# Edge layers of a graph network on one core: 38 instead of 29 tiles fetched as rows, 45 instead of 54 gathered by matmul

## The reference, cut to what matters

```python
def _gine_layer(x, src, dst, edge_attr, eps, We, be, W1, b1, gamma, beta, W2, b2):
    e = edge_attr @ We + be                      # edge_attr: one number an edge
    m = relu(x[src] + e)
    agg = segment_sum(m, dst, num_segments=N)
    h = ((1.0 + eps) * x + agg) @ W1 + b1
    h = (h - mean(h)) * rsqrt(var(h) + 1e-5) * gamma + beta     # over the nodes
    return relu(relu(h) @ W2 + b2)
```

## Time and profile before

| | us |
|---|---|
| median of three runs | 1023.49 (1018.66 to 1024.08) |
| the profiled execution, its own time | 1026.04 |
| its span, first to last instruction | 1024.3 |
| PE busy in the span | 875.0 |
| VectorE busy | 692.1 |
| ACT busy | 499.2 |
| POOL busy | 333.7 |

### The profile page before, as it was taken

The page is one execution under the profiler, slowest core; times in us unless marked ns, Lnnn a source line. Parts: engine busy times, 40 slices in busy tenths (PEclk is TensorE's granted clock), DMA queues, the critical chain, the costliest instruction groups (busy, mean ns, idle before and its releaser), DMA issues.

```text
span 1024.3 us, 13343 instructions
## 1 busy us (share of the span) xinstructions
PE 875.0 (85%) x3642; PEld 624.8 (61%) x3642; DVE 692.1 (68%) x1228; ACT 499.2 (49%) x966; POOL 333.7 (33%) x286
## 2 busy tenths in 40 slices
PE   3979768678969999974999998999999988999793
PEld 2666245456747777753666765676655865667572
DVE  7997635576964646476887577964898569875414
ACT  2386004344534313345775566754776467743421
POOL 3000724567011123335360255503652064502100
PEclk9989557898969999996999999999999999999897
DMA  4413525878314130414683177812886058721001
GB/s 104 143 32 95 140 77 164 247 206 273 132 42 173 40 114 0 135 62 107 164 202 86 37 180 188 218 42 64 187 221 191 4 142 217 196 55 42 1 1 50
DMA packets 58198, 122.16 MB, mean 119 GB/s; under 512 B 8025, under 2 KB 21627, under 8 KB 58134
## 3 DMA queue, kind: packets, MB, share of 16 engines
q0 software_dynamic: 20048, 52.18, 21.5%
q1 hardware_dynamic: 35061, 63.82, 20.2%
q10 hardware_dynamic: 3024, 5.31, 1.4%
HBM read 105.56 MB, written 15.73 MB: 118 GB/s over the span
## 4 chain that ended last, share of the span: by engine, by line
PE 71%; DVE 16%; ACT 5%; issue 4%; DMA 1%; another core or an unknown queue 1%; SPq 0%; DVEq 0%; ACTq 0%
PE ps L908 14%; PE ps L653 12%; PE ps L885 10%; PE ps L924 6%; PE ps L940 6%; PE ps L847 5%; PE ps L796 5%; PE ps L772 4%; PE ps L755 2%; DVE z_parts L1581 2%; ACT slot_recs L995 2%; PE ps L744 1%; PE ps L645 1%; PE ps L659 1%; PE ps L679 1%
## 5 line engine op out<-in xcount | busy, mean ns | idle before, releaser
L908 PE MATMUL ps<-z_parts,onehot_dst 128*125 128x512 f32 x664 | 207.5, 418 | 12.6 <-DVE z_parts L1581 9.5
L653 PE MATMUL ps<-w,xT 128*125 128x512 f32 x660 | 175.0, 419 | 12.7 <-DVE w L1224 4.9
L1581 DVE SCALAR_TENSOR_TENSOR z_parts<-ps,z_parts 128x512 fp32r<-128x512 f32 x216 | 147.6, 687 | 50.8 <-ACT z_parts L1124 43.3
L1124 ACT ACTIVATE z_parts<-ps 128x512 fp32r<-128x512 f32 x216 | 129.1, 598 | 87.5 <-PE ps L885 78.1
L885 PE MATMUL ps<-x_parts,gather_lhs 128*128 x432 | 143.9, 419 | 32.1 <-DVE x_parts L1558 21.0
L908 PEld LDWEIGHTS ps<-z_parts,onehot_dst 128*125 128x125 f32 x664 | 111.6, 188 | 81.4 <-issue 63.0
L653 PEld LDWEIGHTS ps<-w,xT 128*125 128x125 f32 x660 | 126.5, 197 | 49.2 <-issue 19.9
L604 POOL DMA_INDIRECT gathered<-rel_rows,rowi x83 | 88.6, 1068 | 161.3 <-DMA rel_rows<-x_cur 96.1
L619 POOL DMA_INDIRECT queued<-node_rows,srci x60 | 96.1, 1601 | 104.0 <-ACT queued L1058 88.2
L885 PEld LDWEIGHTS ps<-x_parts,gather_lhs 128*128 128x128 f32 x432 | 81.4, 195 | 65.8 <-issue 48.9
L584 POOL TENSOR_TENSOR w<-w_stage,w 128x512 fp32r<-128x512 f32 x36 | 47.9, 1360 | 179.4 <-ACT w L957 179.4
(11 more groups left out here) (240 smaller groups left out, 1204.1 us busy)
## 6 DMA issues: line engine op xcount, KB each, us to landing
w_stage<-in_weights SPq DMA_DIRECT2D x22, 1024.0 KB
onehot_dst<-onehot_rows SPq DMA_DIRECT2D x80, 250.0 KB
onehot_rows<-onehot_dst ACTq DMA_DIRECT2D x20, 250.0 KB
gather_lhs<-edge_src_rows SPq DMA_DIRECT2D x8, 432.0 KB, 8.6
node_rows<-work SPq DMA_DIRECT2D x20, 160.0 KB, 2.0
queued<-node_rows,srci POOLq DMA_INDIRECT x116
node_rows<-work SPq DMA_DIRECT2D x20, 90.0 KB, 2.0
rel_rows<-rel_rows_out SPq DMA_DIRECT2D x10, 160.0 KB, 1.9
```

Source lines behind the costliest of these rows:

```text
L653: mm = pe.matmul(ps[0:R, bank, :], lt[:, a, k, n * R:(n + 1) * R], w[:, b, k, :], start=first and k == 0 and (a, b) == THREE[0], stop=last ...
L908: mm = pe.matmul(ps[0:R, d, :], S[:, j // SK % SR, j % SK, :], Z[:, g % ZR, a, :], start=False, stop=False, skip_group_check=True)
L1124: nc.scalar.activation(Z[:, g % ZR, HI, :], of, ACT.Relu).then_inc(z_hi, 1)
L1581: v.scalar_tensor_tensor(out=Z[:, g % ZR, LO, :], in0=of, scalar=0.0, in1=Z[:, g % ZR, HI, :].bitcast(F32), op0=ALU.max, op1=ALU.subtract) ...
```

## The change

Two constants are new: `TP` = 45, the number of tiles that PE gathers in an edge layer, and `FL` = `TE` - `TP` = 38, the number that POOL fetches. `TF` and `TL` stay what they were where the tiles are made, counted and one-hot encoded. So tiles 45 to 53, full ones, are now fetched. Their gather columns in `L` are still built and loaded, and not used. `ORDER` becomes 7 tiles of PE, then 38 pairs of one PE tile and one fetched tile. Sets on ACT become 19 a layer (15 before), adds on VectorE 19 (14 before). Sources and signs for the fetches (`srci`, `srcf`, `sgf`) are made for 38 columns.

```diff
+TP = 45
+FL = TE - TP
...
-LEAD = TF - 3 * (TL // 2)
+LEAD = TP - FL
 ORDER = [*range(LEAD)]
-for q in range(TL // 2):
-    a, b = LEAD + 3 * q, TF + 2 * q
-    ORDER += [a, b, a + 1, b + 1, a + 2]
-ORDER += range(TF + TL // 2 * 2, TE)
+for q in range(FL):
+    ORDER += [LEAD + q, TP + q]
 STEP = {t: i for i, t in enumerate(ORDER)}
-SETS = (TL + 1) // 2
-ADDS = TL // 2
+SETS = (FL + 1) // 2
+ADDS = FL // 2
...
-        srci = sb("srci", [P, TL], I32)
+        srci = sb("srci", [P, FL], I32)
...
                     if k >= QR:
-                        gp.wait_ge(z_made, l * TE + STEP[TF + k - QR] + 1)
+                        gp.wait_ge(z_made, l * TE + STEP[TP + k - QR] + 1)
                     gp.indirect_dma_start(Q[k % QR][:, :], None, xb_d, row).then_inc(q_in[k % QR], 16)
...
-                for k in range(TL):
+                for k in range(FL):
                     queue_rows(l, k)
...
                     t = ORDER[i] if i < TE else TE
-                    if t < TF:
+                    if t < TP:
...
-                    while k < TL and STEP[TF + k] - 14 <= i:
+                    while k < FL and STEP[TP + k] - 14 <= i:
                         queue_set(l, k)
                         k += 2
...
-                    v.tensor_scalar(SSL[:, g % 2, k, :], iota5[:, :], sgf[:, t - TF + k:t - TF + k + 1], None,
+                    v.tensor_scalar(SSL[:, g % 2, k, :], iota5[:, :], sgf[:, t - TP + k:t - TP + k + 1], None,
...
-            mixed = dlo[:, LEAD:LEAD + 5 * ADDS].rearrange("p (q m) -> p q m", m=5)
+            mixed = dlo[:, LEAD:TE].rearrange("p (q m) -> p q m", m=2)
             v.tensor_copy(dlo[:, 0:LEAD], dlf[:, 0:LEAD])
-            v.tensor_copy(mixed[:, :, 0:5:2], dlf[:, LEAD:TF].rearrange("p (q m) -> p q m", m=3))
-            v.tensor_copy(mixed[:, :, 1:5:2], dlf[:, TF:TF + 2 * ADDS].rearrange("p (q m) -> p q m", m=2))
-            link(v.tensor_copy(dlo[:, LEAD + 5 * ADDS:TE], dlf[:, TF + 2 * ADDS:TE]))
+            v.tensor_copy(mixed[:, :, 0], dlf[:, LEAD:TP])
+            link(v.tensor_copy(mixed[:, :, 1], dlf[:, TP:TE]))
...
-                    while k < TL and STEP[TF + k] <= i + 2:
+                    while k < FL and STEP[TP + k] <= i + 2:
                         queue_add(l, k)
                         k += 2
```

More of the change, by code:

```diff
@@ L896, in _ @@
                         g = l * TE + j
-                        if r >= TF:
-                            if r == TF or r % PK == 0:
+                        if r >= TP:
+                            if r == TP or r % PK == 0:
                                 rest = rest_word(r // PK)
@@ L901, in _ @@
                         else:
-                            last = max(t for t in ORDER[:min(i, TE - 1) + 1] if t < TF)
+                            last = max(t for t in ORDER[:min(i, TE - 1) + 1] if t < TP)
                             d = field(wd if r // PK == last // PK else old, 6 * (r % PK), 7, NT - 1)
@@ L1056, in queue_set @@
                 if k >= QR:
-                    act.wait_ge(z_made, l * TE + STEP[TF + k - QR] + 1)
-                nc.scalar.activation(Q[k % QR][:, :], WEB[:, :], ACT.Copy, scale=wt[:, TF + k:TF + k + 1])\
+                    act.wait_ge(z_made, l * TE + STEP[TP + k - QR] + 1)
+                nc.scalar.activation(Q[k % QR][:, :], WEB[:, :], ACT.Copy, scale=wt[:, TP + k:TP + k + 1])\
                     .then_inc(q_set, 1)
@@ L1111, in _ @@
                     g = l * TE + i
-                    if t < TF:
-                        act.wait_ge(gat_done, l * TF + t + 1)
+                    if t < TP:
+                        act.wait_ge(gat_done, l * TP + t + 1)
                         of = ps[:, 5 + t % 3, :]
                     else:
-                        c = l * ((TL - 1 - (t - TF) % QR) // QR + 1) + (t - TF) // QR + 1
-                        if (t - TF) % 2 == 0:
-                            act.wait_ge(q_in[(t - TF) % QR], 16 * c)
-                        else:
-                            act.wait_ge(q_add, ADDS * l + (t - TF) // 2 + 1)
-                        of = Q[(t - TF) % QR][:, :]
+                        c = l * ((FL - 1 - (t - TP) % QR) // QR + 1) + (t - TP) // QR + 1
+                        if (t - TP) % 2 == 0:
+                            act.wait_ge(q_in[(t - TP) % QR], 16 * c)
+                        else:
+                            act.wait_ge(q_add, ADDS * l + (t - TP) // 2 + 1)
+                        of = Q[(t - TP) % QR][:, :]
                     if g >= ZR:
@@ L1375, in _ @@
             v.tensor_scalar(rowi[:, :], rowf[:, :], -1.0, 0.0, ALU.add, ALU.max)
-            link(v.tensor_scalar(srcf[:, :], rowf[:, TF:TE], float(N + 1), None, ALU.is_ge))
-            link(v.scalar_tensor_tensor(out=srcf[:, :], in0=rowf[:, TF:TE], scalar=float(2 * N + 1), in1=srcf[:, :],
+            link(v.tensor_scalar(srcf[:, :], rowf[:, TP:TE], float(N + 1), None, ALU.is_ge))
+            link(v.scalar_tensor_tensor(out=srcf[:, :], in0=rowf[:, TP:TE], scalar=float(2 * N + 1), in1=srcf[:, :],
                                         op0=ALU.is_ge, op1=ALU.add))
-            v.scalar_tensor_tensor(out=sgf[:, :], in0=srcf[:, :], scalar=-float(NT * P), in1=ps[:, 7, TF:TE],
+            v.scalar_tensor_tensor(out=sgf[:, :], in0=srcf[:, :], scalar=-float(NT * P), in1=ps[:, 7, TP:TE],
                                    op0=ALU.mult, op1=ALU.add)
-            link(v.scalar_tensor_tensor(out=srcf[:, :], in0=srcf[:, :], scalar=-float(N), in1=rowf[:, TF:TE],
+            link(v.scalar_tensor_tensor(out=srcf[:, :], in0=srcf[:, :], scalar=-float(N), in1=rowf[:, TP:TE],
                                         op0=ALU.mult, op1=ALU.add))
@@ L1563, in queue_add @@
                     v.wait_ge(web_in, 16 * (l + 1))
-                v.wait_ge(q_in[k % QR], 16 * (l * ((TL - 1 - k % QR) // QR + 1) + k // QR + 1))
-                v.scalar_tensor_tensor(out=Q[k % QR][:, :], in0=WEB[:, :], scalar=wt[:, TF + k:TF + k + 1],
+                v.wait_ge(q_in[k % QR], 16 * (l * ((FL - 1 - k % QR) // QR + 1) + k // QR + 1))
+                v.scalar_tensor_tensor(out=Q[k % QR][:, :], in0=WEB[:, :], scalar=wt[:, TP + k:TP + k + 1],
                                        in1=Q[k % QR][:, :], op0=ALU.mult, op1=ALU.add).then_inc(q_add, 1)
```

8 lines of the change are left out of this document (4 added, 4 removed).

## The result

The changed kernel took **1047.85 us** in the median of four runs (1039.9 to 1055.3) against 1023.78 us for the kernel before in its four. The ratio is **1.023**, 95% interval 1.016 to 1.030: slower, by 1.6 to 3.0%. On a second chip, where the kernel before takes 988 us, the repeat gave 1.0196 (1.013 to 1.026). Both kernels have now and then an execution in a slower state; such executions are left out of every ratio. The profiled execution of the changed kernel is the slowest of its four: 1055.3 us, 29.3 us above the profiled execution of before.

The account below looks back on a forecast made before the run. PE and VectorE, both nearly full, were taken as the bound, passing to POOL with the transfers. Pace -6.4 and weight loads +4.5 gave -1.9 us against 1026.04, or 1021.5 us as a median; range 1002 to 1040.

Parts of the forecast that it names:

- the start of a layer: Layers 1 to 3: first fetched tile needed five steps earlier, arriving just in time at 597.15 us in layer 1; cost zero.
- the weight loads: Layers 1 to 3: more fetched tiles delay the 1 MB load after the tenth one-hot group; +1.5 us each, +4.5 us.
- the sum: Whole kernel: -6.4 + 4.5 = -1.9 us against the profiled 1026.04, so 1024.1; as a median 1021.5 us.
- Pace: Mixed part of the four edge layers: 0.84 us a step instead of 0.857, -1.6 us a layer, -6.4 us over four.
- The ends of the range, 0.785 and 0.89: Mixed steps: 0.785 us if only POOL's issue limits, 0.89 by the transfers; -5.7 and +2.2 us a layer.
- I cost this at zero, but its cover is gone: Second fetched tile in layers 1 to 3: no cost, but each 0.5 us late costs 0.5 us in three layers.
- C: Mixed part: transfers become the bound, pace 0.89, plus 3 us at each of three weight loads; +17.6, 1041 us; chance 0.22.
- B: Mixed part: transfers have room, only POOL's issue limits, pace 0.785; -18.4, 1005 us; chance 0.22.
- D: Mixed part: tied engines only change partners, pace stays 0.857, weight stalls grow 2 us in three layers; +4.6, 1028; chance 0.13.
- E: POOL's fetches each held by a VectorE instruction reading two SBUF operands, some 10 us more a layer; 1064 us; chance 0.03.
- Wrong in kind if the layers change by over 4 us each: Four edge layers: a change of over 4 us each, in either sense, would make the forecast wrong in kind.
- if anything outside the four layers moves by more than 2 us: Rest of the program: any move of more than 2 us would make the forecast wrong in kind.

## Why the prediction was wrong

The forecast was 1021.5 us, with 1002 to 1040 as its range, and 1047.85 was measured. Two steps failed: the start of a layer, put at zero, and the weight loads, of which the second in each layer was not in the sum.

- **Pace, -6.4 us: right where nothing disturbs.** 0.84 us a step was forecast, 0.832 measured, adds 3.33 us apart for 3.36; layer 0 gained 1.2 to 1.5 for 1.6. In layers 1 to 3 the calm stretch from 52 to 68 gained even 1.5 us each. The ends of the range, 0.785 and 0.89, both fell.
- **Start of a layer, costed at zero: wrong.** This was the step "I cost this at zero, but its cover is gone". POOL starts 4.4 us after PE, as said, but VectorE goes on 7.2 us after the first issue, not after 5.4: the time at which bytes are through was taken for the time at which their reader may go on. The trace of before had a better number: the last recorded landing of a layer's second fetch is there 6.5 us (layer 1) and 7.3 us (layer 3) after the first issue, and 7.1 in the changed kernel's layer 1. Measured +7.5 us in three layers. The runs whose first fetched tile comes later show it from the other side: 7.2 to 8.8 us for steps 0 to 8, as before.
- **Weight loads, +4.5 us: about right for the load that it priced; the other load was missing.** "In each of three layers" priced one load per layer, the one after the tenth group. Steps 8 to 52 take 5.4 us more in the first pair of traces and 1.9 more in the repeat. What the load itself costs depends on the gain in pace that is taken off. With the forecast's 132 steps x 0.017 us it is 7.7 and 4.2; with 1.7 and 1.6 us a layer, the gain of layer 0 in the same steps, 10.5 and 6.7. So +4.5 was of the right size, and the range given, 0 to 9, is about what was met. But the second load of each layer, after the seventeenth group, was never looked at, because the trace of before shows no wait behind it. Measured **+10.5 us**, and the run that moves this load alone brings 12 of 19 us back. This is the step that failed most.
- **What decides there was named wrongly as well**: the sum counted fetched bytes ahead of the weights. The run with cut loads shows that the same bytes at the same share cost nothing when they do not stand as 1 MB in front of the one-hot group. ACT reads the first load from step 42 on, and where it is late it stops too: 1.13 us in layer 1 of the kernel before, 1.6 to 2.2 us with 50 tiles gathered. So that load can be cut or placed better, but not put off. What stands ahead of the group in its queue, and how fast the engines drain it, sets when it lands; its lead of eight steps sets whether anyone notices. Before, it landed 6.3 to 7.5 us after its issue, just inside that lead, with the engines at 0.94 to 0.96; afterwards PE went on 10.3 us after the issue, 3.5 too late.
- **The sum.** Forecast -1.9; measured in the layers, by layer 0, the start, steps 8 to 52, 52 to 68, 68 to 76 and the rest, -1.4 + 7.5 + 5.4 - 4.5 + 10.5 - 1.0 = +16.5. The rest of the 29.3 us between the two profiled executions is the pair of long issues, 9.6, and some 3 us in small pieces. The repeat, 1.0196 or 19 us, is the better measure of the change.
- **The rivals.** C (1041, transfers the bound) was nearest in time, which is in part luck, and right in kind about the weight loads. Its pace of 0.89 did not come, so its mechanism is not what was measured. B's pace did not come either. D had the sign, about a quarter of the size, and one of the places. E did not come: the accumulating fetch takes 1.73 us in the mean, 1.65 in the repeat and 1.56 at a layer's start, far from 2.2. Two of the sums are off by 0.1 to 0.2 us (B is -18.3, C +17.8), which changes nothing. The Trainium skill, page SBUF — State Buffer, section "SBUF: two separate sides", with its exclusive lock on the port pair that VectorE and GpSimd share, would have made E the likeliest case; the trace did not bear that out before and does not after.
- **"Wrong in kind if the layers change by over 4 us each"**: two of four did. So did "if anything outside the four layers moves by more than 2 us": the first aggregation moved by 9.6, though not by the change. The range was too narrow since its upper end took 3 us at one load in each layer, and nothing for the start.

The Trainium skill, page DMA: Bandwidth & Descriptors, section "Queues, rings and completion order", says that a DMA engine takes turns between the queues that have work and works through one queue's descriptors in order. The traces agree in kind: with denser fetches on POOL's queue what is on SP's lands later (8.2 to 10.0 us against 6.3 to 7.5), and there the packets of the group begin, at 794.49 in layer 2, when 368 of the 512 of the 1 MB in front of it have started.

## What to carry to other kernels

A trace tells nothing of a cover until it is gone: for every small transfer that an engine needs soon, compare the time from issue to need with the time from issue to landing (7.0 against 6.3 to 7.5 us here, before the change), and do so for each place in the loop, not only for those where a wait is seen. Here the lead was eight steps, and the move of one large load, or its cutting into parts with the small ones between, was worth 12 to 22 us with the new order (1.0196 to 1.0071 and to 0.9975) and nothing that these runs can tell with the old. How much of that is the order in the queue and how much the spreading in time is open. Changing the mix of work between engines is worth little when all are at 95%: nine tiles less on PE bought 1.2 to 1.5 us in the undisturbed layer.

## What was not expected of the hardware

- An accumulating indirect fetch of 256 KB takes about 1.66 us of all DMA engines, a plain one 0.86 (worked out from the queue shares of the changed kernel and of its version with plain fetches).
- Through both a stall and a calm stretch the engines moved 302 to 309 GB/s at shares of 1.02 to 1.09. The share alone does not tell whether anyone waits.
- A program may show two POOL issues of 5.10 and 4.56 us back to back at one place, in some traces and not in others, in both kernels; it comes with 9 us in the stage. What makes it come was not tried.
